# A hybrid attention and tree-FFN kernel: TensorE's projection steps in two parts over two slots, their readers one slot behind, a new table of slots, and x loaded a phase ahead

## What is computed

```python
x = x + attn_a(layernorm(x), qkv_w, qkv_b, out_w, out_b)     # 16 heads of 16, full softmax, biases
x = x + ffn(layernorm(x), Wq, routers, leaf_values, Wout_w, Wout_b)
x = x + attn_b(layernorm(x), Wq, Wk, Wv, Wo)                  # RoPE, causal softmax, no biases
x = x + ffn(layernorm(x), ...)
# ffn: gate = sigmoid((x @ Wq.T) @ routers.T) gives 255 branch probabilities,
#      the products down an 8-level tree give 256 leaf probabilities,
#      out = (leaf @ leaf_values) @ Wout.T + bias
```

## Time and profile before

| what | value |
|---|---|
| median of 3 runs | 1309.46 us (1306.55 to 1310.61) |
| the profiled execution's own time | 1311.34 us |
| its span | 1309.6 us |
| PE, DVE, ACT, POOL busy | 1169.9, 936.4, 718.1, 336.9 us |
| mean granted clock of TensorE | 0.95 |

### The profile page before, as it was taken

The page is one execution under the profiler, slowest core; times in us unless marked ns, Lnnn a source line. Parts: engine busy times, 40 slices in busy tenths (PEclk is TensorE's granted clock), DMA queues, the critical chain, the costliest instruction groups (busy, mean ns, idle before and its releaser), DMA issues.

```text
span 1309.6 us, 19252 instructions
## 1 busy us (share of the span) xinstructions
PE 1169.9 (89%) x6416; PEld 565.2 (43%) x6416; DVE 936.4 (72%) x2599; ACT 718.1 (55%) x1458; POOL 336.9 (26%) x386
## 2 busy tenths in 40 slices
PE   5799999998998989989899998989889898888986
PEld 3123344344443544345343453435444354444544
DVE  3767786857777758876787667886768867787743
ACT  3165755655465555665556555565545665464551
POOL 3011203313241121412315113240323316262220
PEclk9599999999898989999899998999989999998997
DMA  7250310312004130131302213032120402011000
GB/s 204 50 129 1 88 27 17 113 50 73 25 25 121 33 90 10 43 103 33 98 1 83 64 49 81 2 113 66 48 50 2 145 17 86 13 46 53 18 17 17
DMA packets 60977, 75.33 MB, mean 58 GB/s; under 512 B 6064, under 2 KB 46672, under 8 KB 60880
## 3 DMA queue, kind: packets, MB, share of 16 engines
q1 hardware_dynamic: 58768, 73.81, 20.2%
q0 software_dynamic: 2112, 0.30, 0.1%
HBM read 12.45 MB, written 4.19 MB: 13 GB/s over the span
## 4 chain that ended last, share of the span: by engine, by line
PE 59%; DVE 16%; ACT 6%; issue 6%; SPq 5%; DMA 4%; POOL 2%; POOLq 0%; DVEq 0%
PE ps_work L1170 16%; PE ps_out L1087 11%; PE ps_max L1031 9%; PE ps_key L1063 9%; PE ps_work L1196 8%; SPq L447 5%; PE ps_work L1141 4%; DVE ps_max L789 4%; DMA q_stack<-q_part 3%; ACT probs L700 2%; DVE neg_max L793 2%; DVE scratch L944 2%; DVE scratch L947 2%; DVE scratch L916 2%; PE ps_work L1097 2%
## 5 line engine op out<-in xcount | busy, mean ns | idle before, releaser
L700 ACT ACTIVATE probs<-ps_key 128x512 f32<-128x512 f32 (+3 forms) x1024 | 503.9, 518 | 349.7 <-PE ps_key L1063 342.4
L1031 PE MATMUL ps_max<-k_stack,q_stack 96*128 96x512 bf16 (+3 forms) x1024 | 358.0, 357 | 68.0 <-DVE neg_max L789 37.9
L793 DVE TENSOR_REDUCE neg_max<-ps_max 128x1 bf16<-128x512 f32 x512 | 328.9, 683 | 85.8 <-PE ps_max L1031 84.5
L1063 PE MATMUL ps_key<-q_stack,k_stack 97*128 97x512 bf16 (+3 forms) x1024 | 354.7, 350 | 23.2 <-ACT probs L700 14.2
L789 DVE CUSTOM_DVE_ANT_0 ps_max<-ps_max,mask_b 128x128 f32<-128x128 f32 (+3 forms) x512 | 245.6, 504 | 125.9 <-PE ps_max L1031 125.7
L1087 PE MATMUL ps_out<-probs,v_ones 128*32 128x512 f32 (+3 forms) x2048 | 244.4, 550 | 0.6 <-POOL probs L601 0.6
L1031 PEld LDWEIGHTS ps_max<-k_stack,q_stack 96*128 96x128 bf16 x1024 | 101.2, 99 | 324.5 <-DVE neg_max L789 91.7
L1063 PEld LDWEIGHTS ps_key<-q_stack,k_stack 97*128 97x128 bf16 x1024 | 101.3, 99 | 148.1 <-ACT probs L700 74.5
L601 POOL TENSOR_SCALAR_AFFINE_SELECT probs<-probs 128x512 f32<-128x512 f32 x128 | 83.7, 654 | 293.8 <-ACT probs L700 293.4
L587 POOL DMA_DIRECT2D q_stack<-shift_rows x64 | 34.7, 543 | 404.8 <-DVE shift_rows L803 320.5
L1141 PE MATMUL ps_work<-ident,scratch 128*128 128x128 f32 x384 | 63.3, 297 | 26.2 <-DMA a_v_bias<-in_a_v_bias 9.7
(11 more groups left out here) (86 smaller groups left out, 1290.4 us busy)
## 6 DMA issues: line engine op xcount, KB each, us to landing
k_stack<-k_part SPq DMA_DIRECT2D x48, 256.0 KB
q_stack<-q_part SPq DMA_DIRECT2D x48, 256.0 KB
k_stack<-k_part SPq DMA_DIRECT2D x96, 128.0 KB
q_stack<-q_part SPq DMA_DIRECT2D x96, 128.0 KB
x_in<-in_x SPq DMA_DIRECT2D x8, 512.0 KB, 4.7
x_again<-in_x SPq DMA_DIRECT2D x8, 512.0 KB, 4.6
x_moved<-x_plain SPq DMA_DIRECT2D x7, 512.0 KB, 3.3
out<-x_causal SPq DMA_DIRECT2D x7, 512.0 KB, 3.2
```

What stands on the lines that cost most here:

```text
L700: act.activation(probs[step % RING][:, j, q0:T], ps_key[slot % 2][:, 0:T - q0], ACT.Exp, scale=SCALE).then_inc(on["exp_done"], 1)
L793: dve.tensor_reduce(out=dst, in_=src, axis=AX_X, op=ALU.max, negate=True)\
L1031: pe.matmul(dst[:, 0:keys], q_stack[n % 2][0:SPLIT_ROWS, h, P * qt:P * qt + P], k_stack[n % 2][0:SPLIT_ROWS, h, 0:keys], start=True, stop= ...
L1063: pe.matmul(ps_key[slot % 2][:, 0:T - q0], k_stack[n % 2][0:STACK_ROWS, h, P * kb:P * kb + P], q_stack[n % 2][0:STACK_ROWS, h, q0:T], star ...
```

## The change

The tables name for each step of TensorE the slots of its parts and, apart from that, the slot of the engine that reads it: `(step, half, (slots of TensorE's parts), slot)`. The two early and late finishing tables become one. Matmul steps (project_out, gates, mix, values, heads) are cut in two: half of the rows, or one of the two contractions of heads, in each of two consecutive slots; the reader stands a slot behind the second. Turning steps are one part, their reader one slot behind. Nearly all preparing and finishing steps move to other slots. `load_x` for phase n+2's element is issued at slot 10 of phase n and no longer for n+1 at slot 0.

```diff
-FINISH_EARLY = (
-    (1, "bias_input", 0), (3, "bias_input", 1), (9, "turn_attended", 0), (11, "turn_attended", 1),
-    (14, "project_out", 0), (18, "project_out", 1), (19, "moments", 0), (20, "moments", 1), (21, "spread", 0),
...
-FINISH_LATE = (
...
-    (30, "project_out", 0), (34, "project_out", 1), (35, "moments", 0), (37, "moments", 1), (39, "spread", 0),
...
+FINISH = (
+    ("bias_input", 0, (), 1), ("bias_input", 1, (), 3),
+    ("turn_attended", 0, (18,), 19), ("turn_attended", 1, (19,), 20),
+    ("project_out", 0, (21, 22), 23), ("project_out", 1, (23, 24), 25),
+    ("moments", 0, (), 24), ("moments", 1, (), 26), ("spread", 0, (), 27),
+    ("normalize", 0, (), 29), ("normalize", 1, (), 30),
+    ("turn_normed", 0, (31,), 32), ("turn_normed", 1, (32,), 33),
+    ("gates", 0, (34, 35), 36), ("gates", 1, (36, 37), 38),
+    ("leaves", 0, (), 40), ("leaves", 1, (), 42), ("leaves", 2, (), 44), ("leaves", 3, (), 46), ("leaves", 4, (), 48),
+    ("turn_leaves", 0, (50,), 51), ("turn_leaves", 1, (51,), 52),
+    ("mix", 0, (53, 54), 55), ("mix", 1, (55, 56), 57),
 )
...
+    ("heads_k", 0, (9, 10), 11), ("heads_k", 1, (11, 12), 13),
+    ("heads_q", 0, (13, 14), 15), ("heads_q", 1, (15, 16), 17),
...
+    ("values", 0, (SLOTS + 2, SLOTS + 3), SLOTS + 4), ("values", 1, (SLOTS + 4, SLOTS + 5), SLOTS + 6),
...
+def matmul_schedule(n):
+
+    due = {}
+    for slots, _, step, i, m in sorted(work_of(n), key=lambda w: w[1]):
+        for part, slot in enumerate(slots):
+            due.setdefault(slot, []).append((step, i, m, part))
     return due
...
-                    if n + 1 < PHASES and not causal(n + 1):
-                        load_x(n + 1)
+                    else:
+                        load_x(1)
+                if slot == 10 and n + 2 < PHASES and not causal(n + 2):
+                    load_x(n + 2)
```

More of the change, by code:

```diff
@@ L1160, in turn_leaves, with rows @@
                 turn_tiles(leaf_probs[(LEVELS - 1) % 2], i, bank)
-            def rows(turned, weight, i, bank, width, read):
-                pe.wait_ge(on["turned"], count.of("turned"))
-                take(bank, read)
-                for t in range(2):
+            def rows(turned, weight, i, bank, width, read, parts, full):
+                if 0 in parts:
+                    pe.wait_ge(on["turned"], count.of("turned"))
+                    take(bank, read)
+                for t in parts:
                     tile = slice(P * (2 * i + t), P * (2 * i + t + 1))
@@ L1185, in values, with project_out, gates @@
-            def values(m, i, n, bank):
-                rows(turned_heads, weights["b_v" if causal(m) else "a_v"], i, bank, D, "values_ready")\
-                    .then_inc(on["values_full"], 1)
+                if 1 in parts:
+                    last.then_inc(on[full], 1)
+            def project_out(m, i, n, bank, parts):
+                rows(turned_block, weights["b_o" if causal(m) else "a_o"], i, bank, D, "x_ready", parts, "added_full")
+            def gates(m, i, n, bank, parts):
+                rows(turned_block, gate_w, i, bank, NODES, "gates", parts, "gates_full")
@@ L1189, in heads, with mix, values, step @@
+            def mix(m, i, n, bank, parts):
+                rows(turned_block, leaf_w, i, bank, D, "x_ready", parts, "added_full")
+            def values(m, i, n, bank, parts):
+                rows(turned_heads, weights["b_v" if causal(m) else "a_v"], i, bank, D, "values_ready", parts, "values_full")
             def heads(which):
-                def step(m, i, n, bank):
+                def step(m, i, n, bank, parts):
                     weight = weights[("b_" if causal(m) else "a_") + which]
-                    pe.wait_ge(on["turned"], count.of("turned"))
-                    take(bank, "raw_ready")
-                    for k in range(KC):
+                    if 0 in parts:
+                        pe.wait_ge(on["turned"], count.of("turned"))
+                        take(bank, "raw_ready")
+                    for k in parts:
@@ L1196, in step @@
                         last = pe.matmul(bank[:, :], weight[:, k, P * i:P * i + P], turned_heads[:, k, :],
                                          start=(k == 0), stop=(k == KC - 1))
-                    last.then_inc(on["heads_full"], 1)
-                return step
-            program(core, dict(turn_attended=turn_attended, turn_normed=turn_normed,
-                                          turn_leaves=turn_leaves, project_out=project_out, gates=gates, mix=mix,
-                                          values=values, heads_k=heads("k"), heads_q=heads("q")),
-                    opening, closing)
+                    if 1 in parts:
+                        last.then_inc(on["heads_full"], 1)
@@ new lines, in heads @@
+                return step
+            steps = dict(turn_attended=turn_attended, turn_normed=turn_normed, turn_leaves=turn_leaves,
+                         project_out=project_out, gates=gates, mix=mix, values=values,
+                         heads_k=heads("k"), heads_q=heads("q"))
+            whole = range(2)
+            for step, i in PREPARE_FIRST:
+                if step in steps:
+                    steps[step](0, i, -1, bank_of[step, i, 0, -1], whole)
+            opening()
+            for n in range(PHASES):
+                due = matmul_schedule(n)
+                for slot in range(SLOTS):
+                    core(n, slot)
+                    for step, i, m, part in due.get(slot, ()):
+                        steps[step](m, i, n, bank_of[step, i, m, n], (part,))
```

83 lines of the change are left out of this document (38 added, 45 removed).

## The result

The changed kernel takes 1394.83 us, the median of 4 runs (1386.94 to 1401.74); the kernel before, in the same series, 1310.03 (4 runs). The ratio is 1.065, with a 95% interval of 1.058 to 1.072: it is slower, by 85 us, where 28 less were forecast. The profiled execution took 1401.74 us, with a span of 1400.0.

What follows compares the result with a forecast made beforehand. TensorE was taken to bound the kernel, with 12 us of a plain and 17 of a causal phase waiting or running slowly; the phase terms summed to -28, so 1311.3 - 28 = 1283 us (1282 for the median), range 1266 to 1300.

Steps and rivals of the forecast that it cites:

- the pile of slots 24 to 32: VectorE's load in slots 24 to 32 makes TensorE wait: 3.9 us a plain phase, 3.1 a causal one.
- slots 18 to 21: Moved turn_attended and project_out wait for ScalarE: 2.5 us a causal phase, 0.9 a plain one with a causal preparation.
- 34: Slot 34: both turned copies needed two slots after turn_normed 1, 0.6 us in every phase from 1 on.
- 55 to 58: turn_out and turn_max want mix's banks one slot after their readers: 0.8 us plain, 1.2 causal.
- 11: Slot 11: heads_k 1 waits for the reader of heads_k 0's bank, 1.15 us, 1.1 in causal phases; phases 0 to 14.
- the price of nothing for cutting: Cutting the projections: the same matmuls at 0.865 us a part, nothing added; bound 2 us a phase.
- 40 to 50: Plain: 0.7 us waiting for q_stack and 1.2 for leaves; causal: 3.5 us of waiting behind maxima and leaves.
- rest and clock: Plain: scattered 1.0 us and 1.3 for a short clock fall; causal: 0.5 and 1.5 of slow clock.
- the slower rival: The pile at slots 24 to 32 pulls the clock down: +3.2 us a phase, 1330 us; chance 0.20.
- the credit: Causal phases 5 to 11: 14.4 us of waits and slow clock against 17.2, -2.8 each, -11 together.
- the q_stack rival: Keep shares engines with stack copies, q_stack lands 2.7 us later at slot 40: +22, 1304 us; chance 0.15.
- The even rival: Parts between units keep VectorE and ScalarE fed, waits of slots 24 to 32 halve, clock stays up: 1252 us; chance 0.15.

Runs made afterwards that it cites:

- x ahead: The kernel before with only x of phase n+2 loaded at slot 10 of phase n: 1303.44 us, ratio 0.998.
- uncut: The changed kernel with both parts of each projection in the second of its two slots, reader still one slot behind: 1330.75 us, ratio 1.019.
- uncut, old finishing: The changed kernel's preparation, uncut, with the two finishing tables of the kernel before and x ahead: 1297.6 us, ratio 0.993.
- turn_normed later: The uncut kernel with turn_normed two slots later and gates two and one later: 1316.04 us.
- the cut in the old slots: The kernel before with x ahead and every projection cut, second half and reader one slot later: 1312.72 us, ratio 1.005.
- the waits cleared singly: The changed kernel, made whole in three runs: project_out 1 and mix 1; project_out 0 and gates 0; heads_k 1: 1377.83, 1382.77, 1381.29 us.
- the clear cuts: The changed kernel with heads_k 1, both of project_out, gates 0 and mix 1 whole in their second slot, all else cut: 1341.96 us.

## Why the prediction was wrong

The parts, as measured: x ahead -3, new preparation -6, new finishing +33, cut +64, which makes 1306.5 + 88 = 1395. This is a chain from kernel to kernel, so that it adds up is no evidence in itself; with the finishing changed first it would be +40 and -12. The forecast had -28 for all of it. The steps of it that failed are the sizes of the new waits in its sum (the pile of slots 24 to 32 above all, then slots 18 to 21, 34, 55 to 58 and 11), and the price of nothing for cutting, behind which most of these waits stand.

Forecast and measured excess of a phase in us, by stretches; in each cell plain (4, 6, 8, 10), causal (5, 7, 9). The last two columns are the kernels that take the cut back, and then the new finishing too. In the forecast the slow clock stands in the row of the rest, in the measured columns in the row where it falls.

| slots | forecast plain, causal | after | uncut | uncut, old finishing |
|---|---|---|---|---|
| 0 to 8 | 0.5, 0.4 | 1.3, 1.2 | 1.4, 1.3 | 1.3, 1.3 |
| 9 to 12 | 1.15, 1.1 | 1.9, 1.7 | 0.3, 0.3 | 0.3, 1.1 |
| 18 to 23 | 0.9, 2.5 | 1.6, 5.1 | 0.8, 2.5 | 2.6, 2.3 |
| 24 to 33 | 3.9, 3.1 | 6.6, 6.1 | 7.4, 5.7 | 2.5, 2.1 |
| 34 to 39 | 0.6, 0.6 | 1.2, 3.5 | 0.5, 1.3 | 1.8, 3.7 |
| 40 to 50 | 1.9, 3.5 | 1.9, 4.0 | 1.9, 4.3 | 1.3, 1.8 |
| 51 to 58 | 0.8, 1.2 | 2.1, 2.6 | 0.3, 0.6 | 2.0, 0.6 |
| rest and clock | 2.3, 2.0 | 1.1, 0.8 | 1.2, 1.5 | 0.7, 0.8 |
| sum | 12.0, 14.4 | 17.6, 24.9 | 13.8, 17.5 | 12.5, 13.6 |

**The cut** was priced at nothing for itself, and as matmuls that is near enough: 20 us appear when heads are cut and lie in slot 11, and cuts without a bank or copy to wait for cost 9 to 11 in all. But its waits were entered as if they belonged to the new slots. Its price is that a first half takes its bank and asks for its turned copy a slot before the whole step would; project_out 1 takes one ahead of turn_out, so that turn_max is left with the bank whose reader is latest. The places of this were in the working (slots 11, 18 to 21, 26, 34, 55 to 58), each found at its place; all but turn_max's at slot 26 came out larger than forecast.

**The failed step in size: waits of one hop.** At slot 11 exp and copy were taken as 0.49 + 0.60 and a signal, 1.15; measured 1.5. The missing term is the hop of 0.41 us between the key's start and exp's, of which 0.22 is the key's own time, and the last signal took 0.14 for some 0.06. Over 15 phases this is 5 us. The hop could be read in the kernel before, from a key matmul of phase 4 and its exp:

```profile
372.88 0.38 PE L1063 MATMUL ps_key<-q_stack,k_stack 97*128 97x512 bf16 x1
```

```profile
373.30 0.60 ACT L700 ACTIVATE probs<-ps_key 128x512 f32<-128x512 f32 x1 [0.88 <-PE ps_key L1063]
```

The other places came out larger too: slots 55 to 58 1.7 plain and 1.9 causal for 0.8 and 1.2; slots 34 and 35 1.0 plain and 3.0 causal for 0.6, the causal ones with the slow clock; slots 18 to 23 1.6 and 5.1 for 0.9 and 2.5. That it is the same missing hop in each was not measured.

**The failed step in kind: the pile of slots 24 to 32.** 3.9 plain and 3.1 causal were forecast, with 1.3 and 1.5 for the clock put aside for the whole phase; 6.6 and 6.1 came. The places are right (turn_max 1.09 for 1.4, score 31 0.68 for 1.3), but turn_normed waits 1.8 for 0.8 in phase 4. The mis-sized term there is the normalization beside low_q: the sum added 0.4 us for it, while the row shown for it before the change had 2.42 for two tiles; it took 2.22, against 0.72 without low_q, so 1.5 more, by this estimate most of the wait. The same two tiles meet low_q in phases 2, 4, 6, 8, 10, 12, 13 and 14. In phases 3, 5, 7, 9, 11 and 15 low_q is over, and VectorE stands idle 0.57 us for rstd, which takes GpSimd 1.03; the sum had no term for it, and turn_normed waits 1.6. No run moves low_q or rstd, so what they cost is read from the trace and not tested. Behind the wait stands the slow clock with the gates at half speed, 10.2 us of it in each of phases 5, 7 and 9. That is the slower rival, priced at 3.2 a phase; its mechanism is found, but by itself it does not explain the loss: over the span the clock's cost (busy time at the lower level, by half) rose only from 56 to 64 us, since stretches behind slots 26 and 40 went. Two thirds of the pile come with the new finishing table, as the last column shows.

**Causal phases: the credit.** 5.2 us at slots 26 to 29 and 7.2 near slot 40 were to shrink to 3.1 and 3.5. They did not vanish but moved, to slots 19 to 23 (ScalarE's copies, 5.1 with the slow clock behind) and 31 to 35. Phases 13 and 14, credited with 5 together, lost 18. In phase 0 the wait for the row of shifts fell from 2.79 us to 0.38, but a key matmul 12 us earlier waits 1.49 for exp, with slow clock behind it, and 1.2 of the 4.5 us were won.

**Right, in part by luck:** the q_stack rival is wrong: keep landed 2.9 to 4.7 us after its issue, and it asked for more than 5. That the wait for q_stack is gone (0.7 forecast) is luck: in phase 4 TensorE came to slot 40 33.7 us after slot 17 and not 30.1. With turn_normed later it came at 29.8, and the last copy held it for 1.53 us, until 31.3, close to the 30.8 forecast. Slots 40 to 50 came out at 1.9 in plain phases as forecast, but 0.7 of the forecast was that wait, so the leaves cost 1.9 for 1.2; the 4.0 for 3.5 in causal ones is fair. Right without luck: no wait for x_in behind the start, and the q and values parts at no cost.

**The even rival** (parts between units keep VectorE and ScalarE fed) is refuted by the cut in the old slots, 9 us slower and not faster.

**What the clock costs.** In the project_out 0 shown above, by starts, the step took 3.27 us for 1.83, of which 2.9 lay at the lower clock. The Trainium skill, TensorE: Matmul & The Clock Gate, HAM oscillation — how this bites in real kernels, counts throttled time at half its length as loss; the trace agrees, with 1.44 us lost in 2.9.

**Open:** some 18 of the 90 us of span are busy time at full clock, matmuls that are paced and not held; no view here tells by whom. Whether the waits cleared singly give less than the clear cuts do together (43 and 53) is not settled by these runs; why the slow stretch grows in plain phases and shrinks in causal ones is not known.

## What to carry to other kernels

Cutting a step in two moves its first half forward: before doing so list, for each first half, who read its buffer last and who writes its input, and how late they are in the trace (one slot was enough behind the reader of heads_k 0 and too little behind that of project_out 1). Price a hop between engines from start to start in the trace (here 0.4 us to ScalarE), not from durations. And one table for phases of different load hurts both; here old finishing with new preparation and one moved turning gave 1294 us, 1.1% under the kernel before.

## What the runs showed of the hardware

The stretch at the lower clock behind slot 31 of phase 4 went from 3.4 to 6.8 us when a wait twenty slots ahead of it was taken away, while those of phase 5 went from 13.7 to 10.2 in all; the time at the lower clock doesn't follow the waits in proportion. In one execution, of the kernel with project_out 1 and mix 1 whole, TensorE ran at a granted clock of 0.95 wherever it was not at the lower level, here by stretches of phase 5:

```profile
462.00:484.00 22.00, 20.36 (x108) 9.74 (x108) 13.89 (x48) 11.75 (x26) 5.45 (x7) 0.95 0.00 1
484.00:498.00 14.00, 11.91 (x73) 6.38 (x72) 10.14 (x28) 9.79 (x20) 6.18 (x7) 0.95 0.98 220
```

Two normalized tiles took 2.22 us beside GpSimd's subtractions, as shown, and 0.72 without them, in DVE's timeline of phase 5:

```profile
502.71 0.72 DVE L936 TENSOR_SCALAR scratch<-x_plain,spread,rstd 128x256 f32<-128x256 f32 x2
```

In phase 4 singly they took 1.07 and 1.24 us beside subtractions of 1.14 and 1.19, and each ended 0.15 us behind one of these, as if it had to wait until GpSimd was through. The Trainium skill, GPSIMD Engine Reference, 1. Specifications, has the two engines share their ways to SBUF, with contention where VectorE's instruction reads two tensors or runs in a mode with two ports; this one reads one tensor, and no view here tells its mode.
